# Attention on one core: the last chunk's row sums move to VectorE, more key tiles are split into pairs

## The reference

```python
q = _mxfp4_matmul(x, wq_codes, wq_scales) + bq      # 16 heads of 128
k = _mxfp4_matmul(x, wk_codes, wk_scales) + bk
v = _mxfp4_matmul(x, wv_codes, wv_scales) + bv
scores = jnp.einsum('bqhd,bkhd->bhqk', q, k) / jnp.sqrt(jnp.float32(HEAD_DIM))
attn = jax.nn.softmax(scores, axis=-1)
out = jnp.einsum('bhqk,bkhd->bqhd', attn, v).reshape(B, S, NUM_HEADS * HEAD_DIM)
return _mxfp4_matmul(out, wo_codes, wo_scales) + bo
```

## Time and profile before

| | us |
|---|---|
| median of 3 runs | 2734.06 (2732.32 to 2735.7) |
| the profiled execution, its own time | 2721.14 |
| its span in the trace | 2719.3 |
| TensorE busy in the span | 2605.1 (96%) |
| VectorE busy | 2052.9 (75%) |
| ScalarE busy | 1620.1 (60%) |
| GpSimd busy | 2142.2 (79%) |

### The profile page before, as it was taken

One profiled execution on the slowest core, in us unless ns is written; L12 is line 12 of the kernel. 1 busy time (PEld: TensorE's weight loads), 2 busy tenths in 40 slices (PEclk: granted clock), 3 DMA queues, 4 the chain that ended last, 5 costly groups with the idle time before them and its releaser, 6 DMA issues. The chain is left out here.

```text
span 2719.3 us, 32388 instructions
## 1 busy us (share of the span) xinstructions
PE 2605.1 (96%) x11005; PEld 1864.1 (69%) x11006; DVE 2052.9 (75%) x2908; ACT 1620.1 (60%) x1892; POOL 2142.2 (79%) x1109
## 2 busy tenths in 40 slices
PE   7986999899999999999999999999999999997998
PEld 2333676777777777777777777777777777765765
DVE  6767667588888888888888888888888888887221
ACT  2334233377767776776777677667767776774122
POOL 2543889289988998998899899889989988997333
PEclk9998999999999999999999999999999999998999
DMA  2001566100000000000000000000000000004521
GB/s 69 0 0 64 159 168 165 51 12 5 13 9 12 9 5 16 4 12 1 20 8 5 16 4 9 5 16 7 10 17 4 9 5 9 1 18 104 212 62 47
DMA packets 76398, 92.57 MB, mean 34 GB/s; under 512 B 9342, under 2 KB 64881, under 8 KB 75986
## 3 DMA queue, kind: packets, MB, share of 16 engines
q1 hardware_dynamic: 73266, 83.36, 10.6%
q0 software_dynamic: 2976, 7.22, 0.9%
HBM read 64.43 MB, written 27.04 MB: 34 GB/s over the span
## 5 line engine op out<-in xcount | busy, mean ns | idle before, releaser
L1917 DVE TENSOR_TENSOR at_top<-at_psum_s,at_top 128x512 f32<-128x512 f32 x960 | 662.6, 690 | 212.4 <-ACT at_prob L1824 191.1
L1824 ACT ACTIVATE at_prob<-at_psum_s 128x1024 f32<-128x1024 f32 x512 | 521.1, 1018 | 450.1 <-PE at_psum_s L876 445.9
L2045 POOL TENSOR_TENSOR at_p_lo<-at_prob,at_p_hi 128x1024 fp32r<-128x1024 f32 x256 | 615.2, 2403 | 2.0 <-ACT at_p_hi L1838 2.0
L1906 DVE TENSOR_TENSOR at_prob<-at_prob,at_psum_m 128x1024 f32<-128x1024 f32 x512 | 603.4, 1210 | 0.0
L1830 ACT ACTIVATE at_prob<-at_prob 128x1024 f32<-128x1024 f32 x512 | 537.7, 1050 | 10.3 <-DVE at_prob L1906 7.2
L2074 POOL TENSOR_TENSOR at_acc<-at_acc,at_prob 128x1024 f32<-128x1024 f32 x189 | 452.8, 2396 | 83.5 <-ACT at_prob L1830 72.6
L1739 PE MATMUL at_psum_o<-at_prob,at_v 128*128 128x512 f32 x1024 | 483.4, 595 | 2.3 <-DVE at_oT_lo L1938 1.4
L2078 POOL TENSOR_TENSOR at_acc<-at_acc,at_prob 128x1024 f32<-128x1024 f32 x189 | 453.5, 2399 | 0.0
L874 PE MATMUL at_psum_s<-at_q_hi,sw_gate_up_hi 128*128 128x512 f32 x1024 | 402.1, 393 | 4.4 <-DVE sw_gate_up_lo L1898 4.4
L875 PE MATMUL at_psum_s<-at_q_lo,sw_gate_up_hi 128*128 128x512 f32 x1024 | 400.7, 391 | 0.0
L876 PE MATMUL at_psum_s<-at_q_hi,sw_gate_up_lo 128*128 128x512 f32 x1024 | 400.3, 391 | 0.0
(11 more groups left out here) (342 smaller groups left out, 4440.0 us busy)
## 6 DMA issues: line engine op xcount, KB each, us to landing
ef_gate_up<-in_ef_gate_up SPq DMA_DIRECT2D x8, 1024.0 KB, 14.0
at_wq_split<-lf_pieces SPq DMA_DIRECT2D x8, 512.0 KB, 2.9
at_wk_split<-lf_pieces SPq DMA_DIRECT2D x8, 512.0 KB, 4.1
at_wv_split<-lf_pieces SPq DMA_DIRECT2D x8, 512.0 KB, 3.0
at_wo_split<-lf_pieces SPq DMA_DIRECT2D x8, 512.0 KB, 4.6
ef_down<-in_ef_down SPq DMA_DIRECT2D x8, 512.0 KB, 13.5
ef_rows_in<-ef_zeros SPq DMA_DIRECT2D x23, 128.5 KB, 8.3
ef_rows<-ef_rows_in SPq DMA_DIRECT2D x23, 128.5 KB, 2.2
```

The lines of the kernel that those rows point to most:

```text
L1824: nc.scalar.activation(pair(u, c, half), psum_s[:, 2 * half:2 * half + 2, :], ACT.Copy).then_inc(kept, 1)
L1906: nc.vector.tensor_tensor(part, part, psum_m[:].unsqueeze(1).to_broadcast([P, 2, BT]), ALU.subtract).then_inc(shifted, 1)
L1917: nc.vector.tensor_tensor(top[:, u % 2, :], psum_s[:, t, :], top[:, u % 2, :], ALU.max).then_inc(maxed, 1)
L2045: nc.gpsimd.tensor_tensor(p_lo[:, at, :], part, p_hi[:, at, :].bitcast(F32), ALU.subtract).then_inc(p_lo_ready, 1)
```

## The change

1. `PAIRED` goes from (2, 2, 2, 2) to (3, 2, 3, 2): in chunks 0 and 2 three tiles of v and of the probabilities are split pairs and one stays plain. `split_hi` and `split_lo` get a second instruction there, for one tile (128x512).
2. The sums: on GpSimd chunk 3 is no longer added in two steps and folded. GpSimd adds the sums so far (`acc2`) once onto the first two tiles of chunk 3 in `prob` itself, after they are split; VectorE then sums the four tiles of chunk 3 in four reduces (`add_last`), each over a quarter of the queries (128 queries, 4 tiles), that read tiles 2048 bytes apart. Three stand at c = 1, one at c = 2. The result lies in the idle half of `top`; `acc` is gone, `ones` shares `acc2`.
3. `sum_rows` on TensorE moves from ahead of `weigh` to behind it at c = 2. On GpSimd `split_lo` moves ahead of the adds in chunks 0 and 3.
4. The running maximum begins with the maximum of tile 1's scores and tile 0's copy in `prob`, instead of a copy and a maximum: one VectorE instruction of 128x512 less for each unit.
5. `keep` of chunk 3 now waits for the four reduces of two units ago; `take_v` waits ahead of its copy where a job has both kinds of tiles.

```diff
-    PAIRED = (2, 2, 2, 2)
+    PAIRED = (3, 2, 3, 2)
+    SPLITS = tuple((n + 1) // 2 for n in PAIRED)
...
+            def acc(u):
+                return top[:, (u + 1) % 2, :]
...
-                        pe.wait_ge(p_lo_ready, u * CH + c + 1)
                         at = PAIR_AT[c % 2]
                         for t in range(PAIRED[c]):
+                            if t % 2 == 0:
+                                pe.wait_ge(p_lo_ready, splits_to(u, c) - SPLITS[c] + t // 2 + 1)
...
-                        if c == 2 and 2 <= u < U + 2:
-                            sum_rows(u - 2)
...
                             weigh(pu, pc)
                         if c == 0 and 1 <= u <= U:
                             spread_top(u - 1)
+                        if c == 2 and 2 <= u < U + 2:
+                            sum_rows(u - 2)
...
-                            act.wait_ge(summed, ((u - 2) * CH + c + 1) * 2)
+                            if c < CH - 1:
+                                act.wait_ge(summed, ((u - 2) * CH + c + 1) * 2)
+                            else:
+                                act.wait_ge(sum_ready, TPB * (u - 1))
...
-                                if half == 0:
-                                    split_hi(eu, ec)
+                                if half < SPLITS[ec]:
+                                    split_hi(eu, ec, half)
...
-                            if c == 0 and t == 0:
-                                nc.vector.tensor_copy(top[:, u % 2, :], psum_s[:, t, :]).then_inc(maxed, 1)
-                            else:
+                            if c == 0 and t == 1:
+                                nc.vector.tensor_tensor(top[:, u % 2, :], psum_s[:, t, :], prob[u % 2][:, 0, :],
+                                                        ALU.max).then_inc(maxed, 2)
+                            elif c > 0 or t > 0:
...
+                    def add_last(u, piece):
+                        if piece == 0:
+                            dve.wait_ge(summed, (u + 1) * CH * 2)
+                            dve.wait_ge(exp_done, (u + 1) * CH * 2)
+                        q = bass.ts(piece, P)
+                        nc.vector.tensor_reduce(acc(u)[:, q], prob[u % 2][:, KT - KPC:KT, q].rearrange("p t q -> p q t"),
+                                                AX.X, ALU.add).then_inc(sum_ready, 1)
...
-                        if c == CH - 1:
-                            pool.wait_ge(summed, n + 2)
-                            if u >= 1:
-                                pool.wait_ge(w_ready, jobs["sum", u - 1] + 1)
-                            nc.gpsimd.tensor_tensor(acc[:], acc2[:, 0], acc2[:, 1], ALU.add).then_inc(sum_ready, 1)
+                        else:
+                            split_lo(u, c)
+                            pool.wait_ge(p_lo_ready, splits_to(u, c))
+                            pool.wait_ge(summed, n)
+                            nc.gpsimd.tensor_tensor(pair(u, c, 0), pair(u, c, 0), acc2[:], ALU.add).then_inc(summed, 2)
```

52 lines of the change are left out of this document (32 added, 20 removed).

## The result

The changed kernel takes **2822.36 us** (median of 3, 2820.76 to 2824.54) where the kernel before takes 2734.06. The ratio is **1.0327**, with a 95% interval of [1.0306, 1.0347]: 88 us slower. The prediction had the sign as the likeliest, but its time (2738.6) and its range (2730 to 2780) are both too low.

The account below looks back on a forecast made before the run. It took TensorE to bound the kernel while nobody else is late. Pairs −21.8, the wait for `out_lo` +24.8 and the end +1.5 gave +4.5 us on 2734.06: 2738.6 us, range 2730 to 2780.

Parts of the forecast that it names:

- What bounds the kernel: Steady attention: TensorE's work sets the time (busy 1867.86 of 1873 us); the first `weigh`'s wait for `out_lo` is the danger.
- Part 1, the pairs: TensorE, c = 2 and c = 0: each converted tile saves 0.17 us, 128 tiles, −21.8 us if TensorE stays the bound.
- Part 2, the reduce: VectorE's four new reduces: 0.68 us each, 0.61 from start to start; upper end 1.02 and 0.95.
- The walk: Unit 20, c = 1: three reduces and ScalarE's split delay `out_lo`, so TensorE waits 0.49 us ahead of `weigh`.
- the first rival: VectorE's reduces: hops cost 0.34 us each, the wait for `out_lo` is 1.40 us, total +41.6, 2775.7 us; chance 0.36.
- The lead: VectorE's step c = 1 begins with TensorE's output just before 1116.61; no lead comes back, the 0.49 us wait repeats.
- Units 5 and 6: First reduce waits for GpSimd's last sum, 0.2 us (0 to 1.2): 0.65 us of wait, 16 units, 10.4 us.
- Unit 1: v projections bind `out_lo`, VectorE's idle 1.43 us covers the reduces: 0.44 us of wait, 7 units, 3.1 us.
- "No wait" in units 3 and 7: Two k projections stand ahead of `weigh` on TensorE, VectorE gets only one `at_k_lo` of 0.66 us more: no wait.
- The other parts: The dropped copy (0.68 us of VectorE) saves nothing; the attention's end costs +1.5 us (0 to 2.4, long reduce 3.8).
- The second, no wait: VectorE late by less than 0.19 us, only unit 1 and the end cost: −17.2, 2716.9 us; chance 0.07.
- The third, GpSimd and the reduces: GpSimd and VectorE's reduces slow each other, 0.5 us a reduce, 2 us of wait: +60 us, 2794 us; chance 0.04.

Follow-up runs that it names:

- experiment 11: Changed kernel, but GpSimd sums all chunks, VectorE folds two tiles by two reduces behind `out_lo`, third pair only in chunk 2: ratio 1.0060 to the kernel before.
- experiment 8: Changed kernel with split pairs for two of four tiles in every chunk again, the four reduces kept: ratio 1.0290 to the kernel before.
- experiment 6: Changed kernel with reduces of 4 columns (most row sums left out) and ScalarE's `q_hi` ahead of the new one-tile split: ratio 0.9968 to the kernel before.
- experiment 1: Changed kernel, but each reduce reads 512 adjacent elements of one tile (sums over neighbouring queries): ratio 1.0088 to the kernel before.
- experiment 2: Changed kernel, but each reduce adds only two tiles, making 256 sums from 512 elements: ratio 1.0084 to the kernel before.
- experiment 5: Changed kernel, but each reduce makes only 4 of its 128 sums, order, waits and pairs kept: ratio 1.0038 to the kernel before.

## Why the prediction was wrong, point by point

**What bounds the kernel.** Right: TensorE, as long as nobody is late, and the wait of the first `weigh` for `out_lo` as the place. 74.7 us of TensorE's waits are there.

**Part 1, the pairs.** The size was right: units 3 and 7, where nothing waits, are 0.33 us shorter for two tiles, and 0.19 for one (experiment 11). What it missed is the condition, which it stated as "if TensorE stays the bound": in light units 0, 4, 5 and 6 TensorE waits for VectorE, and experiment 8 shows the pairs at a gain of nothing there. −21.8 went into the sum as if it were certain. Where nobody waits, in experiment 6, a light unit is 0.27 us shorter than before and not 0.34: c = 2 and c = 0, with the pairs, are 0.24 and 0.16 shorter, c = 1 and c = 3 are 0.05 and 0.08 longer.

**Part 2, the reduce: the step that failed.** The forecast took "the lower end, since L1931 is the same operation on the same number of elements", 0.68 us and 0.61 from start to start. Measured are 1.076 and about 1.00. What decides is how the operand is read, not which operation reads it, and the row with a stepped operand was the nearer one: its price of 0.34 us for 512 elements came out at 0.40. Experiment 1 gives the term its weight: some 65 of the 88 us. Of the two statements of the Trainium skill ("Vector Engine (DVE) Microarchitecture Reference", section 5.2, "Measured stream behaviour on trn2") that the prediction set beside each other, each holds for its own case: experiment 2 is the exception (two places, full rate, 0.698), and the changed kernel's four places pay the rule's price, 1.076 against an estimate of 1.03. A reduce over four tiles is not the exception, and its being one word written for several read doesn't make it so.

**The walk, and what it left out.** With the right length, the first rival's walk is 1.40 us of wait. TensorE stood idle for 1.86 in unit 20 (`weigh` began 4.60 us after the scores of c = 2; where it waits for nobody, in experiment 6, it is 2.73). Three things are missing:

- *The lead.* VectorE began `shift` 1.43 us after the scores of c = 1, not 0.99. The walk took its start from the trace of before, on the reason that VectorE's step begins with TensorE's output. In units 0 and 4, which follow a unit with k projections, it no longer does. One step earlier the k projection's lo part (the tile is named `sw_gate_up_lo`) waits for its hi part, and that stands behind ScalarE's new split of one tile. The rows are from the changed kernel; before, this lo part began 0.75 us ahead of the scores of c = 0, here 0.79 behind them:

```profile
1137.51 0.64 ACT L1854 ACTIVATE at_p_hi<-at_prob 128x512 fp32r<-128x512 f32 x1
1138.05 0.67 ACT L1827 ACTIVATE sw_gate_up_hi<-at_psum_w,at_cols 128x512 fp32r<-128x512 f32 x1
1138.76 0.75 DVE L1914 SCALAR_TENSOR_TENSOR sw_gate_up_lo<-at_psum_w,at_cols,sw_gate_up_hi 128x512 fp32r<-128x512 f32 x1 [0.77 <-ACT sw_gate_up_hi L1827]
```

  With long reduces, but the pairs and so the second splits taken back (experiment 8), `shift` begins at 0.99 in units 0, 4, 5 and 6, and the idle time is 1.45 to 1.49: there the walk of the first rival, 1.40, holds. With the splits and short reduces (experiments 1 and 5) it begins at 0.99 as well. So it takes both, the splits and the long reduces. The prediction also never added up VectorE's work in a light unit: 24.10 in the window before, less the copy, plus 4 × 1.00 is 27.4. By this estimate VectorE can't catch up within a unit of 27.5 us, and of the pairs' 0.34 us next to nothing could have come out. But it is not what makes the unit 29.2.
- *Units 5 and 6.* GpSimd's last sum came 0.48 us late in unit 21. The idle time is 2.2 and 2.0 us, where 0.65 was forecast and 1.6 in the rival. In some of these units the clock fell as well. It was not the idle time alone that did it: 13 of the units numbered 5 or 6 have 2.01 to 2.06 us of it, and behind only four of them (units 6, 13, 21 and 30) the granted clock fell. Such a unit is 1.6 us longer (31.12 us, and 29.51 where the clock stayed); behind units 13 and 21 the next unit gives 0.8 of it back, so that the four cost about 5 us. Below are TensorE's first matmul behind the wait of unit 21, its distance to the next ones, and windows with the granted clock (last but two): 0.53 for the 3.4 us behind the idle time, mostly its level of 1.2 GHz (half of full speed). In experiment 1, without such idle times, units 5 and 6 have none of this. Unit 2 itself, the first with reduces, is a case of its own: VectorE's first reduce waits 3.3 us for GpSimd's sum there, and the unit takes 34.28 us in place of 30.09.

```profile
1186.60 1.92 PE L1750 MATMUL at_psum_o<-at_prob,at_v 128*128 128x512 f32 x2 [2.05 <-DVE at_oT_lo L1956]
...
1188.74 0.63 PE L875 MATMUL at_psum_o<-at_p_lo,at_v_hi 128*128 128x512 f32 x1
1189.17 0.63 PE L876 MATMUL at_psum_o<-at_p_hi,at_v_lo 128*128 128x512 f32 x1
```

```profile
1186.60:1190.00 3.40, 3.40 (x6) 2.00 (x7) 3.32 (x4) 3.35 (x4) 2.89 (x2) 0.53 0.00 0
1190.00:1205.00 15.00, 15.00 (x71) 11.51 (x70) 12.42 (x18) 10.42 (x11) 13.77 (x7) 0.99 0.01 1
```

- *Unit 1.* The prediction let the v projections cover the reduces. They don't: a v projection needs the bank that q left, and `q_lo` frees it late (13.8 us in all, shown above).

```profile
1057.42 0.39 PE L874 MATMUL at_psum_w<-at_wv_hi,x_hi 128*128 128x256 f32 x1 [1.35 <-DVE at_q_lo L1914]
```

  Unit 1 lost 1.66 us where 0.10 was forecast (0.44 less the pairs).

**"No wait" in units 3 and 7.** Right.

**The other parts.** The copy is no saving as far as the runs tell. The end was put at +1.5 (up to 3.8) and is +13.0. One part of it is a wait that I had not looked for: with the turn of the sums behind the last `weigh`, VectorE stands still for it ahead of its last shifts,

```profile
2546.61 0.69 DVE L1949 TENSOR_REDUCE at_rsum<-at_psum_w 128x4 f32<-128x512 f32 x1 [3.24 <-PE at_psum_w L1767]
```

where the earlier trace rows is followed by such an inversion without a wait:

```profile
2451.97 0.69 DVE L1931 TENSOR_REDUCE at_rsum<-at_psum_w 128x4 f32<-128x512 f32 x1
```

From the start of `at_oT_lo` to this inversion VectorE now takes 6.0 us in place of 1.7, for the wait and the fourth reduce: 4.3 us of the 13.0. More of it, 8.3, comes in c = 2 of units 62 and 63, which take 9.92 and 12.84 us in place of 6.46 and 7.94. Unit 63 has neither q nor k to project, and so nothing on TensorE to cover the reduces:

```profile
2511.89 2.07 PE L1750 MATMUL at_psum_o<-at_prob,at_v 128*128 128x512 f32 x2 [3.47 <-DVE at_oT_lo L1956]
```

The granted clock is about half for 3.4 us behind the wait of unit 62 (2.04 us) and for 6.8 around this one. The prediction had one light wait for unit 62 and none for unit 63. The other three reduces of the end add 2.0 us more, and 1.5 are made good elsewhere.

**With a short reduce, was the rest right?** Experiment 1 answers: +19 to 28 us, not +4.5. In its trace 15 of them lie in the 60 units and 6.7 at the end. The light units 0, 2 and 4 are 0.20 to 0.27 longer (0.15 forecast), so the split ahead of `q_hi`, which the prediction walked through correctly, is well sized; the step from experiment 5 to 6 shows it alone, 19 us. Units 5 and 6 are 0.76 and 0.32 longer (0.31 forecast) for GpSimd, unit 1 0.48.

**The rivals.** The first had the mechanism and 2775.7 us; it lacked the lost lead, unit 1 and the end. The second, no wait, needed what experiment 6 made: neither reduces nor split ahead, 0.9968. That is 9 us and not its 17: the 60 units are 12.0 us shorter, the end is 4.8 longer. The third, GpSimd and the reduces, did not happen: beside GpSimd the adjacent reduce took 0.677. The sentence of the Trainium skill ("SBUF — State Buffer", "Who interferes with whom"), that on trn2 a reduce never contends with GpSimd, agrees with that; it is the adds that do.

**The range.** Its upper end was the first rival with all else as planned. Each follow-up (lead, clock, bank, turn) had its own place and all point the same way, so they belonged into the upper bound of that rival.

Open stays why experiment 5, with reduces of hardly any length, still has 5.5 of the 13.0 us at the end, and what decides whether the clock falls behind an idle time of 2 us.

## What to carry to other kernels

Before work is moved to an engine with idle time, add up that engine's work over the shortest unit, not over the whole stretch: 84% in the mean was 88% in a light unit, and the four reduces made it as long as the unit had been. Even that is only a lower bound: the unit came out 1.8 us longer than this work, by one wait in its middle. Price a strided read by a row with a strided read, and if no row has the same pattern, take the dearer one; here it cost 0.4 us an instruction and 65 us in the kernel. Then look what stands just ahead of the instruction that the bound engine waits for, on each engine of its chain: the gain of the pairs (0.3%) came out only when the reduces, ScalarE's split and the turn of the sums all stood behind it.

## What the runs showed of the hardware

- A VectorE reduce of 512 elements from SBUF takes 0.677 us when it reads adjacent words, 0.698 when it goes back and forth between two places, and 1.076 between four, whether these are 2048 or 512 bytes apart (1.077). That is 0.78 ns more for each element read. (The one with two places makes 256 sums of two, the others 128 sums of four.)
- An add of two SBUF operands on VectorE waits for the end of a GpSimd instruction that began before it (2.62 us for an add of 0.68), and a GpSimd instruction waits for such an add (4.43 in place of 3.76 us). Reduces, with one SBUF operand, show neither.
- Behind 2.01 to 2.06 us of idle time TensorE's granted clock fell in 4 of 13 units of the changed kernel (0.53 for 3.4 us in unit 21) and stayed at 1.00 in 9; behind the 1.70 to 1.73 us of units 0 and 4 it always stayed.
